# Second cross-attention of a fused eight-stage kernel: scores from high and low F32R parts, keys split on GpSimd

## The reference, cut to what matters

```
q = layernorm(x) @ Wq          (8 heads of 64)
k = ctx @ Wk ;  v = ctx @ Wv
x = x + softmax(q k^T / 8) v @ Wo + bo
```

## Time and profile before

| what | value |
|---|---|
| median of 3 runs | 2406.95 us (2406.39 to 2409.49) |
| the profiled execution's own time | 2405.5 us |
| its span, first to last instruction | 2403.6 us |
| mean granted TensorE clock | 0.961 of full speed |
| TensorE busy, whole span | 2222.6 us (92%) |
| VectorE busy | 1857.5 us (77%) |
| ScalarE busy | 1492.9 us (62%) |
| GpSimd busy | 685.1 us (29%) |

### The profile page before, as it was taken

The page is one execution under the profiler, slowest core; times in us unless marked ns, Lnnn a source line. Parts: engine busy times, 40 slices in busy tenths (PEclk is TensorE's granted clock), DMA queues, the critical chain, the costliest instruction groups (busy, mean ns, idle before and its releaser), DMA issues.

```text
span 2403.6 us, 49297 instructions
## 1 busy us (share of the span) xinstructions
PE 2222.6 (92%) x14668; PEld 1910.2 (79%) x14669; DVE 1857.5 (77%) x4483; ACT 1492.9 (62%) x3090; POOL 685.1 (29%) x926
## 2 busy tenths in 40 slices
PE   7899999999899899995478999999997999979999
PEld 6688888888698788872257888888886888879998
DVE  3688888888976888887975887887888666866666
ACT  5566666665445677767886666666664654636666
POOL 2255546555412122210001111111102442422334
PEclk9999999999999999997589999999998999979999
DMA  8444554445201444430025445454442000114545
GB/s 216 114 137 129 145 144 138 134 140 151 68 0 47 114 133 126 137 111 15 0 72 146 132 134 153 137 145 140 140 132 62 1 1 3 37 53 139 141 140 158
DMA packets 461646, 256.58 MB, mean 107 GB/s; under 512 B 25664, under 2 KB 442332, under 8 KB 461532
## 3 DMA queue, kind: packets, MB, share of 16 engines
q1 hardware_dynamic: 461532, 255.27, 37.7%
HBM read 150.10 MB, written 105.12 MB: 106 GB/s over the span
## 4 chain that ended last, share of the span: by engine, by line
PE 75%; DVE 12%; ACT 6%; issue 5%; POOL 0%; ACTq 0%; DVEq 0%; POOLq 0%
PE ps_o L904 13%; PE ps_s L891 11%; PE ps_p L87 7%; PE ps_p L89 6%; PE ps_p L88 6%; PE ps_t L881 6%; PE ps_o L1474 3%; PE ps_t L1474 2%; PE ps_t L3129 2%; PE ps_s L3111 2%; PE ps_o L3129 2%; PE ps_s L87 2%; ACT a_keys L1022 2%; DVE a_sm L1197 2%; PE ps_s L89 2%
## 5 line engine op out<-in xcount | busy, mean ns | idle before, releaser
L904 PEld LDWEIGHTS ps_o<-a_val,a_pt 128*128 128x128 f32 (+2 forms) x3200 | 413.6, 192 | 35.0 <-issue 8.4
L904 PE MATMUL ps_o<-a_val,a_pt 128*128 128x128 f32 (+2 forms) x3200 | 423.9, 276 | 5.7 <-ACT a_pt L1059 3.6
L891 PE MATMUL ps_s<-a_keys,a_zt 128*128 128x308 f32 (+1 forms) x1024 | 415.7, 492 | 14.6 <-ACT a_keys L1022 9.8
L1031 ACT ACTIVATE a_stage<-ps_p 128x512 f32<-128x512 f32 (+1 forms) x370 | 221.1, 598 | 276.9 <-PE ps_p L89 275.0
L1197 DVE TENSOR_REDUCE a_sm<-a_e 128x16 f32<-128x1232 f32 (+1 forms) x192 | 234.2, 1220 | 183.2 <-ACT a_e L1067 182.7
L1059 ACT ACTIVATE a_pt<-ps_t 128x512 f32<-128x512 f32 (+1 forms) x448 | 225.2, 505 | 151.1 <-PE ps_t L881 149.8
L1022 ACT ACTIVATE a_keys<-ps_p 128x308 f32<-128x308 f32 x603 | 256.7, 427 | 81.8 <-PE ps_p L89 81.4
L881 PE MATMUL ps_t<-ident,a_e 128*128 128x128 f32 (+1 forms) x1600 | 262.8, 277 | 32.9 <-POOL a_e L1214 16.4
L87 PE MATMUL ps_p<-ct_hi,a_mt_hi 96*128 (+1 forms) x603 | 293.0, 486 | 0.0
L1067 ACT ACTIVATE a_e<-a_e 128x1232 f32<-128x1232 f32 (+1 forms) x192 | 203.9, 1062 | 50.9 <-DVE a_e L1189 34.6
L1214 POOL TENSOR_TENSOR a_e<-a_e,a_rs 128x539 f32<-128x539 f32 (+1 forms) x192 | 165.6, 890 | 234.6 <-DVE a_rs L1202 233.2
(11 more groups left out here) (437 smaller groups left out, 4931.6 us busy)
## 6 DMA issues: line engine op xcount, KB each, us to landing
a_vals<-a_stage SPq DMA_DIRECT2D x160, 512.0 KB, 3.5
a_val<-a_vals SPq DMA_DIRECT2D x128, 576.0 KB
f_w<-in_L_ffn_W_dram SPq DMA_DIRECT2D x129, 256.0 KB, 2.7
a_vals<-a_stage SPq DMA_DIRECT2D x40, 416.0 KB
a_val<-a_vals SPq DMA_DIRECT2D x64, 256.0 KB
a_val<-a_vals SPq DMA_DIRECT2D x128, 40.0 KB
x<-in_x_dram SPq DMA_DIRECT2D x8, 512.0 KB, 7.0
out_dram<-x SPq DMA_DIRECT2D x7, 512.0 KB, 6.8
```

The source lines that it names most:

```text
L891: eng.matmul(c.ps_s[:, b, 0:nh * KEYS], zt, keys[:, h0:h0 + nh, :], start=True, stop=True)\
L904: mm = eng.matmul(c.ps_o[:, (i % 2) * P:(i % 2 + 1) * P], self.pt[0:r, n, :], self.val[0:r, i % 2, n, :], start=(n == 0), stop=(n == self. ...
L1031: eng.activation(self.stage[0:n, slot, BANK * (v % 2):BANK * (v % 2) + BANK], bank[0:n, :], ACT.Copy)\
```

## The change

The second attention is built with `split=True` (the others are not; the diff also has a layout in place for 16 heads, which nothing calls). Its scores are three F32R passes: high z by high keys, low z by high keys, high z by low keys. `keys` becomes `keys_hi` and `keys_lo` (F32R, two groups each), `zt` becomes `zt_hi` and `zt_lo`. ScalarE's copy of the turned z goes to `zt_hi`, and VectorE subtracts it from the bank (`split_zt`, once a group, in k = 1 behind the shift). In the loop ScalarE copies the projected keys, unrounded, to one of four places of a ring (`unsplit`), and before it waits until the key four before has been split. GpSimd rounds each from the ring to `keys_hi`, waits for itself, and subtracts to `keys_lo` (`split_keys`). The scores with k = 2 wait for GpSimd's split in place of ScalarE's copy. For the 11 keys ahead of the loop, ScalarE writes `keys_hi` and VectorE subtracts from the bank. GpSimd's bias, root and window copies move behind the splits of tiles 2 and 6; the window copy's wait for the probabilities goes.

```diff
@@ CrossAttention.scores
-        eng.matmul(c.ps_s[:, b, 0:nh * KEYS], zt, keys[:, h0:h0 + nh, :], start=True, stop=True)\
-           .then_inc(self.scores_ready.sem, 1)
+        o, cols = c.ps_s[:, b, 0:nh * KEYS], slice(k * P, k * P + P)
+        if self.split:
+            mm = three_passes(eng, o, [z[:, par, cols] for z in (self.zt_hi, self.zt_lo)],
+                              [self.batch_of(keys, par, k, b) for keys in (self.keys_hi, self.keys_lo)])
...
+        mm.then_inc(self.scores_ready.sem, 1)
@@ tensor, ahead of the loop
             if u >= 5:
                 eng.wait_ge(self.proj_copied.sem, self.proj_copied.at(u - 4))
+                if self.split and u - 5 >= self.vuses:
+                    eng.wait_ge(self.key_split.sem, self.key_split.at(u - 5 - self.vuses + 1))
...
+        if self.split:
+            eng.wait_ge(self.zt_split.sem, self.zt_split.at(1))
+            eng.wait_ge(self.key_split.sem, self.key_split.at(self.lead - self.vuses))
@@ tensor, window
+                    if self.split and k == 2 and j == 1 and not ends:
+                        eng.wait_ge(self.zt_split.sem, self.zt_split.at(2 * w + par + 2))
...
-                        if k == 2:
+                        if k == 2 and self.split:
+                            eng.wait_ge(self.key_split.sem,
+                                        self.key_split.at(self.keys_for(w, par, b, last) + 1))
+                        elif k == 2:
@@ scalar
+    def keep_keys(self, eng, u, bank, n, slot):
+        eng.wait_ge(self.key_split.sem, self.key_split.at(n - self.RING + 1))
+        eng.wait_ge(self.proj_done.sem, self.proj_done.at(u + 1))
+        eng.activation(self.unsplit[:, slot, :, :], bank[:, 0:GCOLS].rearrange("p (b k) -> p b k", b=GT), ACT.Copy)\
+           .then_inc(self.proj_copied.sem, 1)
@@ vector
+    def split_first_keys(self, eng):
+        for u in range(self.vuses, self.lead):
+            g, h = (u - self.vuses) // self.heads, (u - self.vuses) % self.heads
+            eng.wait_ge(self.proj_copied.sem, self.proj_copied.at(u + 1))
...
+            eng.tensor_tensor(self.unit_of(self.keys_lo, g % 2, h), bank,
+                              self.unit_of(self.keys_hi, g % 2, h).bitcast(F32), ALU.subtract)\
+               .then_inc(self.key_split.sem, 1)
+
+    def split_zt(self, eng, g, par, u, slot):
+        eng.wait_ge(self.t_copied.sem, self.t_copied.at(u + 1))
+        eng.tensor_tensor(self.zt_lo[:, par, :], self.core.ps_t[:, slot, :],
+                          self.zt_hi[:, par, :].bitcast(F32), ALU.subtract).then_inc(self.zt_split.sem, 1)
...
         self.ln.vector_stats(eng, 1)
+        if self.split:
+            self.split_first_keys(eng)
+            self.split_zt(eng, 0, 0, 0, 0)
         if self.left:
             self.quant.quantise_weights(eng)
...
                 if not (last and k >= 2):
                     self.shift(eng, t + 2, k % 2, found)
+                if self.split and k == 1 and not last:
+                    u = 1 + self.gcyc * g + 2 * self.uses
+                    self.split_zt(eng, g + 1, 1 - par, u, (1 + self.gcyc * par + 2 * self.uses) % 2)
                 self.residual(eng, t, k)
@@ gpsimd
+    def split_keys(self, eng, u, n, par, h):
+        src = self.unsplit[:, n % self.RING, :, :]
+        hi, lo = self.unit_of(self.keys_hi, par, h), self.unit_of(self.keys_lo, par, h)
+        eng.wait_ge(self.proj_copied.sem, self.proj_copied.at(u + 1))
+        eng.tensor_copy(hi, src).then_inc(self.key_high.sem, 1)
+        eng.wait_ge(self.key_high.sem, self.key_high.at(n - (self.lead - self.vuses) + 1))
+        eng.tensor_tensor(lo, src, hi.bitcast(F32), ALU.subtract).then_inc(self.key_split.sem, 1)
...
+            for i in range(self.WIN):
+                for kind, h, place in self.plan_of(i, last):
+                    if kind == "k":
+                        self.split_keys(eng, self.use(w, place), self.key_number(w, place, last),
+                                        self.key_group(i) % 2, h)
...
+                if i % GT == 2:
+                    self.ln.pool_bias(eng, g)
+                    if self.left and g >= 3:
+                        self.left.root(eng, g - 3)
...
+                    if more and i >= GT:
+                        eng.wait_ge(self.proj_done.sem, self.proj_done.at(self.use(w, v_last) + 1))
+                        self.copy_window(eng, w + 2)
```

More of the change, by code:

```diff
@@ L588 @@
     BLOCKS = -(-KEYS // KBLOCK)
+    RING = 4
     STAGES = 5
@@ new lines, in count_keys, with key_number, keys_for @@
+    @staticmethod
+    def count_keys(plan):
+        return sum(kind == "k" for mine in plan for kind, _, _ in mine)
+    def key_number(self, w, place, last=False):
+        plan = self.tail if last else self.plan
+        before = sum(kind == "k" and p < place for mine in plan for kind, _, p in mine)
+        return self.first - self.vuses + 2 * self.heads * w + before
+    def keys_for(self, w, par, b, last):
+        if not self.in_place:
+            head = sum(self.head_span(b)) - 1
+            for i in range(3) if par == 0 else range(3, 7):
+                for kind, h, place in self.plan_of(i, last):
+                    if kind == "k" and h == head:
+                        return self.key_number(w, place, last)
+            return self.key_number(w - 1, next(place for kind, h, place in self.plan[-1] if kind == "k" and h == head))
+        order = [h for k in range(GT) for h in self.freed_by(k, 1 - par)]
+        h0, nh = self.head_span(b)
+        return self.heads + 2 * self.heads * w + self.heads * par + max(map(order.index, range(h0, h0 + nh)))
@@ new lines, in stage_of, with stored_by @@
+    def stage_of(self, w, u):
+        if not self.in_place or not (isinstance(w, int) and w == 0):
+            return u % self.slots, u // self.slots, self.stage[:, u % self.slots, :]
+        slot, width = u % self.STAGES, self.PART * P
+        places = [self.stage[:, 0, :], self.stage[:, 1, :], self.e[:, 0, 0:width], self.e[:, 1, 0:width],
+                  self.pt[:, 0:width // P, :].rearrange("p i d -> p (i d)")]
+        return slot, u // self.STAGES, places[slot]
+    def stored_by(self, w, turn):
+        if isinstance(w, int) and w == 0:
+            return 16 * turn
+        return 16 * (self.rounds * (w - 1) + self.first_rounds + turn)
@@ L883, in turn_chunks, with scores @@
         mm.then_inc(self.t_done.sem, 1)
-    def scores(self, eng, t, b, zt, keys, first=False):
+    def scores(self, eng, t, b, par, k, first=False):
         c = self.core
@@ L978, in window, with project_next @@
                 par2 = par if n2 == k + 2 else 1 - par
[L979 to L982 removed]
+                plan = iter([what for what in self.plan_of(i, last) if not self.in_place or what[0] == "v"])
+                keys = iter([what for what in self.plan_of(i, last) if self.in_place and what[0] == "k"])
+                def project_next(n=1, scored=False):
+                    for what in islice(keys if self.in_place and scored else plan, n):
                         self.project(eng, w, i, what, last)
@@ L1107, in window, with copy_next @@
                 more = not (ends and k == GT - 1)
-                plan = iter(self.plan_of(i, last))
-                def copy_next(n):
-                    for what in islice(plan, n):
-                        self.copy_proj(eng, w, i, what)
+                plan = self.plan_of(i, last)
+                before = iter([what for what in plan if not self.in_place or what[0] == "v"])
+                scored = iter([what for what in plan if self.in_place and what[0] == "k"])
+                def copy_next(n, keys=0):
+                    for what in islice(before, n):
+                        self.copy_proj(eng, w, i, what, last)
+                    for what in islice(scored, keys):
+                        self.copy_proj(eng, w, i, what, last)
                 if more and H == 8:
@@ L1323, in gpsimd @@
         self.copy_window(eng, 1)
-        if self.next_stats and not self.setup:
+        if self.next_stats and not self.setup and not self.split:
             self.after.split_weights(eng)
```

168 lines of the change are left out of this document (136 added, 32 removed).

## The result

The changed kernel takes **2455.59 us** (median of 4 runs, 2452.80 to 2457.59), the kernel before 2408.22 beside it on the same chip (2406.39 to 2411.10). The ratio is 1.0193, 95% interval 1.0181 to 1.0206: slower by 47 us. The profiled execution took 2457.59 us with a span of 2455.8, that is 52.2 more than the span before.

What follows compares the result with a forecast made beforehand. TensorE was taken as the bound, VectorE next. Seven windows' 45.5 us, 2.0 for the first window's i = 2 and 12.3 for the start gave 59.8 us on 2405.5: 2465 us, range 2436 to 2497.

Steps and rivals of the forecast that it cites:

- The scores: TensorE's score products: three F32R passes take 0.42 us instead of 0.52, saving 1.55 us a window where TensorE waits for nothing.
- The case of 2393 us: Rival: TensorE stays the only bound, splits and start hidden, 12.4 us faster; chance 0.03.
- The split on GpSimd: GpSimd, each key: rounding 0.45 us, subtraction 0.85, 0.19 between dependent instructions; 1.49 us a split, about 34 us busy a window.
- The waits: Scores right behind their projection wait for GpSimd: 2.7 us later in i = 6, 1.6 in i = 2, before contention.
- Contention: GpSimd's and VectorE's SBUF reads: 0.5 us on a split at each wait, 1.0 us on VectorE in the first half.
- The clock: TensorE behind the new gaps in i = 6 and i = 2: each costs 0 to 3.2 us; 1.0 a window taken.
- The rival in which it falls at one wait: Rival: TensorE's clock falls at one wait each window, 2480 us; chance 0.10 shared with falling at both, 2503.
- The window: Loop, eight sequences: first half 21.0 us, second 23.1, clock 1.0; 45.1 instead of 38.6.
- The start: Ahead of the loop: `quantise_weights` begins only after z is split, ends at 796.0, first shift then; 12.3 us on the path.
- GpSimd as the bound: Rival: above 2.2 us a key GpSimd sets the pace and blocks ScalarE; 2485 us at 2.4 a key; chance 0.08.
- the passes as slow as the F32 product: Rival: three passes cost as much as one F32 score product, 0.8 us a window more, 2471 us; chance 0.04.
- the start alone: Rival: splits hidden and only the start lost, 2405 us, no change; chance 0.03.

Runs made afterwards that it cites:

- e1: Changed kernel with the three passes reading only high parts, ScalarE writing the high keys, nothing split: 2402.48 us, ratio 0.9988 to the kernel before.
- e7: Changed kernel with GpSimd's subtraction replaced by three one-input copies of the unsplit keys: 2453.71 us, ratio 1.0197 to the kernel before.
- e3: Changed kernel with twelve unread F32R products of 512 columns on TensorE before the scores b = 1 in i = 6: 2447.9 us, ratio 1.0171.
- e5: Kernel before with only the projection plan altered, head 7 of each group projected a tile ahead of its scores: 2416.48 us, ratio 1.0033.
- e11: Changed kernel with the second group's head 7 projected a tile before i = 6, which keeps one value projection: 2434.55 us, ratio 1.0107.
- e4: Changed kernel with only the two weight reductions ahead of the loop, the rest of the weights' preparation moved to tile 58: 2456.18 us, ratio 1.0215.
- e12: Kernel before with ScalarE copying heads 6 and 7 right behind the exponentials in i = 6, ahead of the turned probabilities: 2408.07 us, ratio 0.9994.
- e2: Changed kernel with head 7 of each group projected a tile ahead of its scores, all splits kept: 2433.64 us, ratio 1.0116 to the kernel before.
- e6: Changed kernel without splits, three passes reading high parts only, head 7 projected a tile ahead of its scores: 2414.25 us, ratio 1.0024.
- e8: Changed kernel with head 7 projected a tile earlier and GpSimd's subtraction replaced by three one-input copies: 2426.26 us, ratio 1.0081.
- e10: Changed kernel with one key projection moved from tile i = 6 to i = 3: 2452.84 us, ratio 1.0187 to the kernel before.
- e9: Kernel before with one key projection moved from tile i = 6 to i = 3: 2411.94 us, ratio 1.0020.

## Why the prediction was right

The forecast, two new waits a window and the stage's weights behind the splits, is what happened: slower, 2455.6 us against 2465. By its steps, measured on the profiled execution:

- **The scores.** Between other passes a triple takes 0.42 us (866.74 to 867.16), as taken; behind a wait 0.53 (906.95 to 907.48). e1 shows 1.25 us a window less on TensorE (1.55 taken), but that only 0.73 of it reach the window: "only where TensorE waits for nothing" was right and mattered more than I had it. The case of 2393 us, TensorE as the only bound, was never open, for e1 without any split stands at 2402.
- **The split on GpSimd.** Rounding 0.44 us (0.45 taken), subtraction 0.79 (0.85), 0.08 between two instructions where I took 0.19 from an instruction that waits for its own predecessor on small tiles. Undisturbed that is 1.31 us a key instead of 1.49; with what VectorE holds up, the two have means of 0.53 and 0.92 us from 841 to 1100 us. GpSimd is busy 30.5 us a window (34 taken).
- **The waits.** i = 6: 3.85 us (4.4 taken; each of the two splits is 0.18 shorter and the contention 0.08). i = 2: 1.15 where the sum had 1.6 + 0.5 = 2.1 and the clock's case up to 3.9. From the end of ScalarE's copy to the scores 1.93 us pass (905.02 to 906.95), near to what I had; but the copy now ended 0.78 us before TensorE was free for the scores (905.80), not 0.13, and this I left out. Both waits are in their places, with the named releaser.
- **Contention.** 0.42 us on the split beside L1353 (0.5 taken). The Trainium skill, "SBUF — State Buffer", in its section on SBUF's two separate sides, has the loser blocked for the other's whole instruction; as the subtraction began 0.28 us after L1353's 0.85, what was left to wait for is at most 0.57, and the 0.42 is 0.15 short of it. In the earlier trace rows 1.15 us is short of 1.29 by 0.14 too, and so is e7's 1.14 of 1.28, so the rule gives the order of the wait and some 0.15 us too much. The whole 0.80 at both places, my upper sum, was not reached.
- **The clock.** It fell at one wait a window. I took 1.0 us a window, e3 measures 1.2. The rival in which it falls at one wait was priced at 2480 on the full 3.2 us each; the fall came, the price did not.
- **The window.** 44.4 us against 45.1: 21.66 (21.0 and the clock's 1.0 taken) plus 22.73 (23.1 taken). The second half is the wait: 2.67 us more gap less 0.7 of products leaves 0.14 unexplained. In the first half errors hid one another, which is luck: the wait was 0.95 too large in the sum, the clock 0.2 too small, and what is left for VectorE's contention and its split of z is 1.4 us (3.66 + 0.1 - 1.15 - 1.2) against 1.0 taken. From the first turned tile to the end 42.8 us were added, against 7 x 6.5 + 2.0 = 47.5.
- **The start** is the one step that failed: "it ends at 796.0, and the first shift starts there", 12.3 us. From the first key projection to the first maxima 6.2 us were added (6.76 to 12.97). I took the 12.36 us of the block as VectorE's work; for 6.25 of them VectorE had waited for GpSimd's reduction (0.60 after), and this share fell away when GpSimd got there first. The execution also has 3.1 us more from first value to first key, at a lower clock. That is no part of the change: these projections took 10.2 us in the changed kernel, in e5 and in e11, 8.6 in e1 to e4 and 7.04 before; e5 and e12 (8.6) change nothing there, and e7, which has the whole change there, took 7.05.

The sum, 59.8 us, is 7.6 over the 52.2 of the profile: 4.7 from the loop and 6.1 from the start, less the 3.1 of the first projections, which bring the number nearer by luck; the other stretches add up to nearly nothing. By the medians, which are what was asked, 58 us were forecast and 47 came. The rivals that the runs put aside: GpSimd as the bound (it waits for ScalarE 52 times), the passes as slow as the F32 product, the start alone (42.8 of the 52.2 us lie in the loop and its end).

What stays open: the price of the contention on VectorE's chain (L1353 has a mean of 892 ns where L1205 had 841), which no run took away, and how e2's window, 41.3 us against 39.3 in e6 with the same plan and no splits, divides. By e8 0.7 of these 2.0 us go with the two-input subtraction. The two splits of z are 1.35 us of VectorE a window and make TensorE wait 0.6 us a window, and behind L1353 beside the window copy it waits 0.9; that these two make up the rest is argued from the waits, not shown by a run.

## What to carry to other kernels

Where two engines have almost the same busy time in a window (here 37.2 and 33.7 of 38.6), price an edit on the first one by removing its cost without the rest of the change, as e1 did: 10 us of TensorE's busy time were worth 3 to 6. When a copy gets a second step on another engine, look first at the consumers that stand right behind their producer, and count the queue in front of the copy as well as the split. A gap is not worth its length: closing the gap in i = 6 gave 0.12 of 0.59 us (e12) and cost 8 us where it was done by piling three projections on two banks (e5).

## What the runs showed of the hardware

- GpSimd's work on 128 x 308 elements: a rounding copy 0.44 us, a subtraction 0.79, 0.08 us from one to the next even where the second waits for the first.
- A copy with one input on GpSimd is held up by VectorE's product with two inputs too, 1.14 us for three pieces against 0.70, and VectorE's z normalisations, which have one input of full size, took 561 to 949 ns where they ran beside GpSimd's subtraction (18 in e2) and 335 where they did not.
- In three places an instruction held up by the other engine took 0.14 to 0.15 us less than what was left of the other's row plus its own undisturbed time (1.15 against 1.29 us before, 1.21 against 1.36 after, 1.14 against 1.28 in e7).
- TensorE's granted clock fell to 0.50 behind all seven idle times of 3.85 us (after) and six of seven of 3.0 us (e10). Behind 1.1 to 1.2 us it stayed at 1.00 in every window before and after, but fell behind 1.14 us twice in e10 and once in e3, and behind 0.9 us once in e2 (at 880.4 us). A short wait is thus no guarantee; what decides it the runs do not show.
- The 5.7 us ahead of GpSimd's first reduction are seen where its data are there first (5.5 to 5.8 us in the profiles of before, e1, e4, e5, e9 and e12) and not where GpSimd waits for them longer than that.
